# Two routing blocks of a four-layer transformer stack: half of the normalisation on VectorE, and the sorted positions worked out inside the attention loop

## What is computed

```python
xn = _layernorm(x, axis=-1)                      # every layer
# layer 1: causal attention with 16 heads and a linear bias, and
gate_probs = softmax(xf @ gate_w.T)              # 8 experts
topk_scores, topk_idx = top_k(gate_probs, 2)
topk_scores = topk_scores / sum(topk_scores)
out[token] = sum over its two experts of score * expert(xn[token])
# layer 3: the same routing (softmax over the two best), beside an
# attention without a softmax: features elu(t)+1, one sum per head
```

## Time and profile before

| | us |
|---|---|
| median of 3 runs (2945.24 to 2947.10) | 2946.78 |
| span of the profiled execution, first to last instruction | 2847.3 |
| median less that span (start and end of the program) | 99.5 |
| TensorE busy | 2442.7 |
| VectorE busy | 2005.6 |
| ScalarE busy | 1823.8 |
| GpSimd busy | 787.6 |

### The profile page before, as it was taken

How to read it: one execution, slowest core, us unless ns; L and a number is a source line. 1 busy time by engine, 2 the same in 40 slices (tenths; PEclk the granted TensorE clock), 3 DMA queues, 4 the chain that set the end, 5 groups by cost and what they waited for, 6 DMA issues and landing times. The chain is left out here.

```text
span 2847.3 us, 76648 instructions
## 1 busy us (share of the span) xinstructions
PE 2442.7 (86%) x30232; PEld 1812.5 (64%) x30232; DVE 2005.6 (70%) x5914; ACT 1823.8 (64%) x3779; POOL 787.6 (28%) x820
## 2 busy tenths in 40 slices
PE   6858999996889999999999899989996658999964
PEld 6745677774556666566656665666664547999943
DVE  5556544444568776877687677877775498999988
ACT  3334555553566666666666667666763488999997
POOL 3325100002133232323232223222222163111167
PEclk9959999997999999999999999999999689999998
DMA  6201355551000000000000000000000014666611
GB/s 211 38 16 40 115 158 160 155 156 56 11 17 15 4 17 17 15 4 17 17 15 4 17 17 17 9 10 13 14 13 7 1 45 156 203 195 202 192 42 51
DMA packets 104306, 175.17 MB, mean 62 GB/s; under 512 B 16273, under 2 KB 73745, under 8 KB 103825
## 3 DMA queue, kind: packets, MB, share of 16 engines
q1 hardware_dynamic: 94608, 153.20, 18.0%
q0 software_dynamic: 8192, 16.79, 2.0%
q10 hardware_dynamic: 1152, 0.27, 0.0%
HBM read 130.50 MB, written 26.74 MB: 55 GB/s over the span
## 5 line engine op out<-in xcount | busy, mean ns | idle before, releaser
L2014 POOL TENSOR_TENSOR l_rinv<-l_ssm,w_neg_half 128x8 f32<-128x8 f32 x128 | 210.2, 1642 | 551.8 <-DVE l_ssm L2305 551.7
L257 PE MATMUL bank<-l_kT,l_qT 32*128 32x128 f32 (+1 forms) x3072 | 355.0, 350 | 8.8 <-DVE l_qm L1382 7.2
L257 PE MATMUL bank<-l_qm,l_kT 32*128 32x128 f32 (+1 forms) x3072 | 350.7, 347 | 6.3 <-DVE l_qm L2215 6.3
L2045 ACT ACTIVATE l_probsT<-bank 128x768 f32<-128x768 f32 x256 | 208.5, 815 | 160.1 <-PE bank L257 159.3
L276 DVE TENSOR_REDUCE l_tops<-bank 128x2 f32<-128x256 f32 (+1 forms) x384 | 196.1, 511 | 119.9 <-PE bank L257 116.5
L2717 DVE RECIPROCAL l_rden<-l_den 128x256 f32<-128x256 f32 x128 | 223.8, 1748 | 30.0 <-ACT l_den L2628 29.4
L893 POOL DMA_INDIRECT back<-sorted_y,pos x128 | 125.6, 981 | 378.7 <-DMA sorted_y<-l_y_tile 347.8
L277 DVE TENSOR_REDUCE l_tops<-bank 128x2 f32<-128x512 f32 (+1 forms) x384 | 227.5, 592 | 0.0
L257 PEld LDWEIGHTS bank<-l_kT,l_qT 32*128 32x128 f32 x3072 | 205.8, 190 | 18.2 <-DVE l_qm L1382 9.3
L257 PEld LDWEIGHTS bank<-l_qm,l_kT 32*128 32x128 f32 x3072 | 202.9, 188 | 8.2 <-DVE l_qm L2215 8.1
L154 POOL TENSOR_TENSOR l_rstd<-l_var,w_neg_half 128x2 f32<-128x2 f32 (+1 forms) x56 | 42.6, 760 | 569.6 <-DVE l_var L149 556.8
(11 more groups left out here) (350 smaller groups left out, 6967.4 us busy)
## 6 DMA issues: line engine op xcount, KB each, us to landing
l_expert<-in_experts SPq DMA_DIRECT2D x72, 768.0 KB, 4.1
l_expert<-in_experts SPq DMA_DIRECT2D x72, 578.0 KB, 3.5
l_x_tile<-sorted_x SPq DMA_DIRECT2D x144, 64.0 KB, 4.1
sorted_y<-l_y_tile SPq DMA_DIRECT2D x144, 64.0 KB, 3.7
l_v_half<-l_v SPq DMA_DIRECT2D x32, 264.0 KB, 3.2
sorted_x<-x_all SPq DMA_DIRECT2D x18, 256.0 KB, 3.9
l_v_half<-l_v SPq DMA_DIRECT2D x32, 132.0 KB, 3.2
l_x<-in_x SPq DMA_DIRECT2D x8, 256.0 KB, 5.0
```

The costliest lines, as they stand in the source:

```text
L257: lasts.append(pe.matmul(bank[:, at:at + n * P], lhs[:, c * P:(c + 1) * P], rhs[:, x0 * P:(x0 + n) * P], start=False, stop=(i == 1), skip_ ...
L2014: pool.tensor_tensor(rinv[:, i, :], ssm[:, i, :], g.neg_half[:, 0:LH], ALU.pow).then_inc(rinv_ready[l], 1)
L2045: Bt.took(act.activation(probsT[:, (j // 2) % 2, 2 * (j % 2):2 * (j % 2) + 2, :], two[:, :, 0:AW], ACT.Exp), rd, use)
```

## The change

1. Of each group of four chunks ScalarE normalises the first two only. VectorE normalises the other two, in `stats_dve`, which gets two more iterations. A new signal `xn_rest` tells TensorE.
2. `rank_dve` is cut into `rank_choice` and five parts of `rank_places`. In the second layer the parts run in steps 1 to 5 of the attention loop, in VectorE's stream behind the maxima (and the keys) and ahead of `qm`. TensorE waits for ROUTED before the first tile of an expert (step 45) and not before the loop.
3. The two counts of the second layer go to PSUM bank 7, which the tiles of the experts use later, and no longer to the banks 4 and 5 of the loop.
4. In the fourth layer all parts follow `rank_choice` directly, in the old order.

```diff
 def turn(j):
     s.xn_ready.wait(pe, j + 1)
+    s.xn_rest.wait(pe, j + 1)
...
-def count_pe(pe, g, q, s, count_banks):
+def count_pe(pe, g, q, s, within, total):
...
 # norm_act
-            for c in range(4 * j, 4 * j + 4):
+            for c in range(4 * j, 4 * j + 2):
                 last = act.activation(q.xn[:, c, :], g.x_all[:, c, :], ACT.Identity, bias=q.shift[:, c:c + 1],
                                       scale=q.rstd[:, c:c + 1])
...
 # stats_dve
-    for j in range(SG + 2):
+    for j in range(SG + 4):
...
+        if j >= 4:
+            s.shift_ready.wait(dve, j - 3)
+            for c in range(4 * j - 14, 4 * j - 12):
+                last = dve.tensor_scalar(q.xn[:, c, :], g.x_all[:, c, :], q.rstd[:, c:c + 1], q.shift[:, c:c + 1],
+                                         ALU.mult, ALU.add)
+            last.then_inc(s.xn_rest.sem, 1)
...
+PLACE_PARTS = 5
+
+def rank_places(dve, g, q, s, ch, within, total, scale, part):
+    CH = q.xn.shape[1]
+    if part == 0:
+        place_weights(dve, q, s, ch, scale)
+        s.products.wait(dve, 3)
+        q.scanned = ch.mark(dve.tensor_copy(q.run[:, 0, :, :], total))
+        q.reach, q.i = 1, 0
+        place_scan(dve, q, ch, 4)
+    elif part == 1:
+        place_scan(dve, q, ch, CH)
+    elif part == 2:
+        place_bases(dve, g, q, ch, total)
+    elif part == 3:
+        place_tiles(dve, g, q, ch, within)
+    else:
+        place_rows(dve, q, s, ch)
...
 # layer1, TensorE
-        turn_banks, logit_banks, count_banks = g.bank[0:2], g.bank[2:4], g.bank[4:6]
+        turn_banks, logit_banks = g.bank[0:2], g.bank[2:4]
+        within, total = Xb[:, 0:CH * E], Xb[:, CH * E:2 * CH * E]
...
-            count_pe(pe, g, q, s, count_banks)
+            count_pe(pe, g, q, s, within, total)
             for part in (("k", 0), ("v", 0)):
                 project(part)
-            s.routing.wait(pe, ROUTED)
             U.wait_taken(pe, ("v", 0))
             for n in range(LAST):
...
                 if n == A0 - 1:
+                    s.routing.wait(pe, ROUTED)
                     turn_tile(0)
...
 # layer1, VectorE
-            rank_dve(dve, g, q, s, ch, logit_banks, count_banks, 1.0)
+            rank_choice(dve, g, q, s, ch, logit_banks)
...
                     values(part_of(n))
+                if 1 <= n <= PLACE_PARTS:
+                    rank_places(dve, g, q, s, ch, by_expert(within), by_expert(total), 1.0, n - 1)
                 if maxima_of(n) is not None:
                     queries_less_maxima(maxima_of(n))
...
 # layer3, VectorE
-            rank_dve(dve, g, q, s, ch, logit_banks, turn_banks, 0.5)
+            rank_choice(dve, g, q, s, ch, logit_banks)
+            for part in range(PLACE_PARTS):
+                rank_places(dve, g, q, s, ch, *(by_expert(b[:, 0:CH * E]) for b in turn_banks), 0.5, part)
```

More of the change, by code:

```diff
@@ L758, in sorting_signals @@
     s.xn_ready, n["xn_ready"] = Signal(sem("xn_ready")), groups
+    s.xn_rest, n["xn_rest"] = Signal(sem("xn_rest")), groups
     s.turned, n["turned"] = Signal(sem("turned")), groups + tiles
@@ L773, in next_layer @@
         s.xn_ready.base += n["xn_ready"]
+        s.xn_rest.base += n["xn_rest"]
         s.turned.base += n["turned"]
@@ L870, in count_pe, with by_expert @@
     flat = q.chosen[:, :, :].rearrange("p c e -> p (c e)")
-    pe.matmul(count_banks[0][:, 0:CH * E], g.w["tri2"][:, :], flat, start=True, stop=True)
-    pe.matmul(count_banks[1][:, 0:CH * E], g.w["ones2"][:, :], flat, start=True, stop=True).then_inc(s.products.sem, 1)
+    pe.matmul(within, g.w["tri2"][:, :], flat, start=True, stop=True)
+    pe.matmul(total, g.w["ones2"][:, :], flat, start=True, stop=True).then_inc(s.products.sem, 1)
+def by_expert(b):
+    return b.rearrange("p (c e) -> p c e", e=E)
 def norm_pool(pool, g, q, s, ch):
@@ L949, in stats_dve @@
                 joined[j - 1] = ch.mark(dve.bn_aggr(q.mv[:, c, :], q.stats[:, c, :]))
-        if j >= 2:
+        if 2 <= j < SG + 2:
             cs = slice(4 * j - 8, 4 * j - 4)
@@ L984, in rank_dve, with place_scan, place_bases @@
                              op1=ALU.mult)
[L985 to L991, removed]
-        dve.tensor_copy(q.run[:, 1 - i, 0:reach, :], q.run[:, i, 0:reach, :])
[L993 to L997, removed]
+def place_scan(dve, q, ch, end):
+    CH = q.xn.shape[1]
+    while q.reach < end:
+        i, reach = q.i, q.reach
+        ch.wait(q.scanned)
+        dve.tensor_copy(q.run[:, 1 - i, 0:reach, :], q.run[:, i, 0:reach, :])
+        q.scanned = ch.mark(dve.tensor_tensor(q.run[:, 1 - i, reach:CH, :], q.run[:, i, reach:CH, :],
+                                              q.run[:, i, 0:CH - reach, :], ALU.add))
+        q.i, q.reach = 1 - i, 2 * reach
+def place_bases(dve, g, q, ch, total):
+    CH, i = q.xn.shape[1], q.i
+    ch.wait(q.scanned)
+    q.placed_at = ch.mark(dve.tensor_tensor(q.spot[:, :, :], q.run[:, i, :, :], total, ALU.subtract))
     ch(dve.tensor_tensor(q.over[:, :, :], q.run[:, i, CH - 1, :].unsqueeze(2).to_broadcast([P, E, CH]),
@@ L1003, in rank_dve, with place_tiles, place_rows @@
     ch(dve.reduce_sum(q.base[:, :], q.ahead[:, :, :], AX.X))
[L1004 to L1009, removed]
+    q.ends = ch.mark(dve.scalar_tensor_tensor(out=q.end[:, :], in0=q.tiles_of[:, :], scalar=float(P), in1=q.base[:, :],
+                                              op0=ALU.mult, op1=ALU.add))
+    ch.wait(q.placed_at)
+    q.placed_at = ch.mark(dve.scalar_tensor_tensor(out=q.spot[:, :, :], in0=q.spot[:, :, :], scalar=-1.0,
+                                                   in1=over_chunks(q.base[:, :], CH), op0=ALU.add, op1=ALU.add))
+def place_tiles(dve, g, q, ch, within):
+    TILES = q.tile_e.shape[1]
+    ch.wait(q.ends)
     past = ch.mark(dve.tensor_tensor(q.passed[:, :, :], g.w["steps"][:, :].unsqueeze(2).to_broadcast([P, TILES, E - 1]),
                                      q.end[:, 0:E - 1].unsqueeze(1).to_broadcast([P, TILES, E - 1]), ALU.is_ge))
-    ch.wait(placed_at)
-    placed_at = ch.mark(dve.tensor_tensor(q.spot[:, :, :], q.spot[:, :, :], within, ALU.add))
+    ch.wait(q.placed_at)
+    q.placed_at = ch.mark(dve.tensor_tensor(q.spot[:, :, :], q.spot[:, :, :], within, ALU.add))
     ch.wait(past)
-    past = ch.mark(dve.reduce_sum(q.tile_ef[:, :], q.passed[:, :, :], AX.X))
-    ch.wait(placed_at)
+    q.past = ch.mark(dve.reduce_sum(q.tile_ef[:, :], q.passed[:, :, :], AX.X))
+def place_rows(dve, q, s, ch):
+    ch.wait(q.placed_at)
     for k in range(TOP):
         n = ch.mark(dve.tensor_tensor(q.at[:, k, :, :], q.hot[:, k, :, :], q.spot[:, :, :], ALU.mult))
-    ch.wait(past)
+    ch.wait(q.past)
     dve.tensor_copy(q.tile_e[:, :], q.tile_ef[:, :])
@@ L2527, in _ @@
             project(1)
-            count_pe(pe, g, q, s, turn_banks)
+            count_pe(pe, g, q, s, *(b[:, 0:CH * E] for b in turn_banks))
             s.routing.wait(pe, ROUTED)
```

5 lines of the change are left out of this document (3 added, 2 removed).

## The result

| | runs | median us | ratio to before, 95% interval |
|---|---|---|---|
| before | 18 | 2946.40 (2941.44 to 2951.85) | |
| after | 18 | 2952.77 (2948.01 to 2960.82) | 1.0020 [1.0012, 1.0027] |

The change makes the kernel slower by 0.2%, some 6 us. The forecast was 2942.9 us, with a range from 2938.5 to 2947.0: the time moved the other way and lies above the range.

The account below looks back on a forecast made before the run. TensorE was taken as busiest, slowed by low clock, serial routing and turns with VectorE. Gains of 6.95 and 0.4 less 3.5 gave 3.85 us off 2946.78, so 2942.9 us, range 2938.5 to 2947.0.

Parts of the forecast that it names:

- Normalisation: Second and fourth layer: TensorE's second group of transposes starts 0.4 us earlier in each, bounds 0 and 0.65.
- GpSimd held by VectorE's pairs: Rival, normalisation: each group's shift up to 0.59 us later, the 0.4 us gains vanish, 2943.7 us; chance 0.12.
- Positions out of the way: Before the second layer's loop: VectorE takes the keys 6.55 us sooner; with normalisation the loop starts 6.95 us earlier.
- the clock rises sooner: Rival, second layer's loop: TensorE's idle stretch goes, four steps gain at high clock, 3.5 us, 2939.4 us; chance 0.15.
- Positions in the loop: Steps 1 to 5: the five parts, partly hidden in VectorE's idle time, cost 3.5 us, bounds 2.5 and 9.1.
- Part 1: Step 2: this part of the positions lasts 1.46 us ahead of `qm`, 0.54 of it hidden; cost 0.9 us.
- Part 3: Step 4: this part of the positions stands ahead of `qm` with no idle time; costs all of 1.5 us.
- GpSimd is held by the maxima of the step before and catches up. Cost 0.: Second layer's loop: scatters wait for ROUTED, near 212.7 us, but all 64 take 81 us and could end by 294.
- The case on the other side: Clock rises later, in the loop: with twelve more steps at 1.2 GHz the change is slower, 2953.5 us; chance 0.06.

Follow-up runs that it names:

- e1: The kernel before, unchanged, run and profiled again; 2946.76 us, ratio 1.0006 to before.
- e4: The changed kernel with its 64 scatters shared over steps 8 to 43, not 0 to 43; 2949.17 us, ratio 1.0019.
- e8: The changed kernel; scatters wait for the previous step's scores, not its maxima (the gate), and are shared over steps 6 to 43; 2934.93 us, ratio 0.9965.
- e10: The changed kernel with only the gate moved: scatters wait for the previous step's scores, not its maxima; 2933.55 us, ratio 0.9965.
- e11: As e8, but with the first tile of an expert in step 54, not 46; 2914.72 us, ratio 0.9895.
- e5: The kernel before with all 64 scatters of the second layer issued in step 43; 2999.98 us, ratio 1.0182.
- e6: The changed kernel with all 64 scatters of the second layer issued in step 43; 2996.47 us, ratio 1.0170.
- e12: The kernel before; scatters wait for the previous step's scores, not its maxima, and the first expert tile is in step 54; 2924.38 us, ratio 0.9929.
- e2: The changed kernel with all positions ahead of the keys again, VectorE's half of the normalisation kept; 2945.53 us, ratio 1.0003.
- e9: As e2, with scatters waiting for the previous step's scores, not its maxima; 2927.43 us, ratio 0.9934.

## Why the prediction was wrong

**Normalisation: right, a little small.** 0.4 us forecast within 0 to 0.65, 0.58 measured in the second layer and 0.56 in the fourth, where the third group's weights are loaded 10.29 us behind the first statistic in e1 and 9.73 in the kernel after. The step that was short: each pair was put behind the end of its `var` (0.13 us behind its start), and starts 0.04 or 0.05 us behind the start. The second pair so runs from 6.75 to 7.35 us behind the first statistic in place of 6.92 to 7.51, and VectorE's pace with the pairs is 1.62 us a group in place of 1.7.

**GpSimd held by VectorE's pairs: did not come.** `rstd` beside the first pair lasts 1.10 us, the one before it 1.04, and the second shift starts 5.99 us behind the first statistic, 6.00 before (155.84 - 149.84). By the Trainium skill ("VectorE: DVE Perf Modes", Mode 2×_2P, with "GPSIMD Engine Reference", Specifications) GpSimd contends with such a pair; no wait near the pair's 0.60 us shows on GpSimd's rows here, at most the 0.06 us on `rstd`.

**Positions out of the way: right.** The keys come 35.5 us behind the first statistic in place of 42.9, 7.35 us sooner (6.95 forecast with the normalisation). The first maxima come 8.7 us sooner, since the clock was for a moment up in the stretch of keys and v (0.80 in 184 to 188); by 192 it was down again. That moment is luck of the execution: e4, e8, e10 and e11 have 0.50 from 184 to 194, and their first maxima come at 40.2 us and not at 38.7, so 7.2 us sooner. The rival "the clock rises sooner" was there for 4 us and then not; it was up to stay near 210, between the forecast 207 and the 212 of before, until it fell in the standstill of the burst.

**Positions in the loop: the sum was about right.** Step 6 comes 60.1 us behind the first statistic (210.55 - 150.42) in place of 66.3 (216.11 - 149.84): 6.1 us ahead, where 3.45 were forecast for this layer (6.95 - 3.5). Of that, 1.4 us (8.7 less 7.35) are the moment of high clock. From the first maxima to step 6 the change needs 21.4 us (189.13 to 210.55) against 18.8 before (197.28 to 216.11): 2.6 us, at the lower bound of the 3.5 (2.5 to 9.1). In e4, e8, e10 and e11, without the moment, step 6 is 3.9 to 4.1 us ahead. Part 1 costs about what was counted: `qm` of step 2 comes 2.28 us behind its first maxima in place of 1.56, so 0.7 later (0.9 forecast). Part 3 was put too high: `qm` of step 4 comes 3.10 us behind in place of 2.60, so 0.5 later and not 1.5. The forecast saw no idle time ahead of that `qm`, but before the change VectorE idles 0.97 us ahead of the keys in front of it, and after it not at all, so that this much of the part is hidden. Timeline of VectorE, first profile:

```profile
211.91 0.69 DVE L1364 TENSOR_TENSOR l_kT<-bank,w_alibi 128x512 f32<-128x512 f32 x1 [0.97 <-PE bank L1186]
```

**The step that failed** is "GpSimd is held by the maxima of the step before and catches up. Cost 0." GpSimd did catch up, and that is what cost: thirteen scatters in a row held TensorE's signals for 12.2 us (to VectorE) and 11.0 us (to ScalarE), and step 8 came 12.3 us further back against before than step 6 (from 6.7 ahead of e1 to 5.6 behind). With the clock down behind it, step 42 stands 10.6 us behind e1, and the third layer 9.4. The last scatter starts at 344.74, and not 3.5 us sooner than 307.06. The forecast asked whether the scatters end in time, never what they do to the others while they are issued. With all scatters out of the steps (e5, e6) the forecast's own sum appears: 4.3 us at the third layer, for 3.45, and 3.5 in the time, for 3.85. Part of the 4.3 is the moment of high clock, which e6 has too, and the 3.5 is of a single round of two executions each, whose intervals overlap.

**A second step failed that stood in no sum:** that the profile shown was typical. 99.5 us between its span and the time, against 1.9 in the profile after, was the warning. In it no signal is late though 38 fall inside a scatter or right behind one. A reader of it alone could not have found the price of a scatter, but could have doubted the execution.

The case on the other side had the sign but not the cause: it had the clock staying down for a dozen steps by parts 1 and 3. The clock was down from 220 to 236, and TensorE had stood still from 220.15 to 230.76 in the burst.

**What stays open.** By which path an indirect DMA holds TensorE's signals isn't shown, nor whether it is its issue or its own transfers that do it: the gate moved both. Why the first profiled execution is free of it is open too. The gathers of the third layer were left as they are: in e12 13 of them still make hand-overs late, by 23.0 us in all. e11 and e12 are 4.7 us apart in their spans and 9.7 in their medians, so the size of the change's gain with the scatters put right is between these, and only partly explained: 2.6 us of it are there at the third layer. The two kernels are not quite alike in their scatters either: e11 has 13 double steps among these 33 and e12 has 7. The normalisation's 0.6 us in each layer is below what the times of e2 and e9 can show.

## What to carry to other kernels

Before work is moved that releases a queue of DMAs, ask how many of them fall due meanwhile, and what is signalled while they go out. Here the changed kernel and e11, which differ only in the place and density of the scatters (and the tiles that wait for them), are 38 us apart; and the change, by itself 6 us slower, gained 5 to 10 us once they were put right. Hold overdue transfers to one a step, start them right behind the signal that the slowest hand-over waits for, and compare span and time of a profile before a sum is built on it.

## What the runs showed of the hardware

- A scatter of GpSimd (indirect DMA, 0.96 us and 0.31 between two) delays TensorE's signals: 26 of 128 hand-overs to VectorE in e1, by 0.83 us in the median and 1.78 at most, each seen 0.4 to 1.2 us behind the end of a scatter; 12.2 us under a row of thirteen; in e6, under the row of 64, the first hand-over by 5.96 us (VectorE idle for 7.28) and the next by 69.6. Gathers in the third layer do the same (13 of 15 hand-overs, 1.5 to 1.8 us); other instructions of GpSimd don't (20 hand-overs of 0.05 us).
- ScalarE sees its own signal of TensorE late too: together with VectorE behind the burst (229.73 and 229.68), 0.7 us behind it in step 10 of e1 (232.10 and 231.38).
- VectorE's signals to TensorE don't suffer: in e1 22 ends of `qm` that TensorE waits for fall inside a scatter and are taken within 0.06 us, as are the 31 of e5, which has no scatters there.
- A scatter begun within 0.3 us of a signal's arrival costs nothing that shows (2.38 to 2.54 us a step, 2.46 without one); a second behind it costs 0.6 to 0.75 us.
- One execution in the profiles of this kernel had none of these delays, and its steps 9 to 42 took 2.46 us with the scatters in them, the same as e5 without.
